# Two-layer convolution: the second image's last four chunks get their statistics from a quadratic form, and two weight loads are issued earlier

## The chip, the core and the metric

The kernel runs on one core of one Trainium2 chip. The metric is device time in microseconds (us): the median of 3 runs, and beside it one profiled execution from which all rows below are taken. Engines are named as the profile names them: PE (TensorE, matmul), PEld (its weight loads), DVE (VectorE), ACT (ScalarE), POOL (GpSimd), SP (SyncE, which here only issues DMAs).

## What is computed

Layer 0 is a bottleneck block with a deformable 3x3 convolution; the change touches it only in the order of two weight loads. Layer 1, cut to what matters, is this, for two images of 1024 channels and 64x64 pixels:

```python
t = jnp.einsum('oc,bchw->bohw', Wt, x)      # 512 channels
p = jnp.einsum('oc,bchw->bohw', Wp, x)
g = jnp.einsum('oc,bchw->bohw', Wg, x)
y = _rbf_kernel(t, p, g)                    # att0 + att1*t + att2*t**2 per image, att from sums of p**k * g
z = jnp.einsum('oc,bchw->bohw', Wz, y)      # 1024 channels
mu = jnp.mean(z, axis=(1, 2, 3), keepdims=True)
var = jnp.mean((z - mu) ** 2, axis=(1, 2, 3), keepdims=True)
zn = (z - mu) * jax.lax.rsqrt(var + EPS)
zn = zn * gn_w[None, :, None, None] + gn_b[None, :, None, None]
return zn + x
```

So no output of an image can be finished before mean and variance over all of that image's z are known.

## The kernel before

The pixels are worked in 16 chunks of 512 (8 for each image). A 1024-channel tensor of one chunk is 8 tiles of 128 channels x 512 pixels, so z is 128 tiles, counted by i; chunk zc holds the tiles 8*zc to 8*zc+7. The matrix products are done in two parts: each operand is split into a rounded high part and the rest, and `product` (L194 to L196) issues three matmuls, high by high, high by low, low by high. ACT makes the high part and DVE the low one.

The program is a hand-written list for each engine, with semaphores between them; every engine works its list strictly in order. The stages in time:

- convolutions of layer 0, then projections of layer 1 (the weights of the projections are loaded into three staging buffers by `stage`, L464 on SP, split by ACT at L699 and DVE at L1081). While the first projections run, DVE and ACT work through a long list of gathered tiles.
- the z stage. For chunk zc+1, while z of chunk zc runs: POOL loads t into the single buffer `tb` (L658), ACT scales it (`y_scale`, L903), DVE multiplies (`y_square`, L1320), ACT rounds y to `yh` (`y_high`, L915), DVE takes the rest `yl` (`y_low`, L1324). PE makes a tile of z with 4 x 3 matmuls into one of six PSUM banks; the first and the last two tiles of a chunk are done as pairs (`z_pair`). ACT copies the tile from its bank to SBUF (`z_evict`, L968), and DVE takes its statistics (`stats`, L1367). z stays in SBUF in a ring of 71 tiles.
- when an image's 64 tiles have their statistics, DVE, PE and ACT combine them (`fin_mean`, L1618 and L1622 on PE, `fin_std`, `fin_scale`). Then for each tile DVE adds the saved input (`add_x1`, L1402), ACT adds the bias (`fin`, L976), SP stores 256 KB (`store_out`, L560).
- for the first image the 64 additions are spread over the second image's z by `adds_by` (L157): after tile 64+x, max(x-3, 3(x-5)/2) of them are done, so 1.5 for each tile. A tile's bias on ACT comes one tile later. Their inputs come through four buffers `xs` of 256 KB (`load_xs`, L549); on SP the load of xs i+4 stands directly ahead of the store of tile i.
- for the second image everything from L1372 on comes behind the last tile of z; its inputs come as pairs of tiles (512 KB) into 16 buffers `xb` and `xt` (`load_x1`, L554).

## Time and profile before

| | us |
|---|---|
| median of 3 runs (lowest, highest) | 2355.5 (2354.93, 2360.31) |
| the profiled execution | 2341.42 |
| its span, first to last instruction | 2339.6 |
| first matmul of z to the end of the last, about | 1900.7 to 2264.4 |
| from there to the end | 75.2 |

A span counts from the first to the last instruction. A row of the timeline has the start, the duration, the engine, the line and what it writes and reads; a bracket tells how long the engine was idle before it and what it waited for. Matmuls overlap in the records: a 128x512 one lasts 0.39 us and the next starts 0.23 us after it. What one costs is the distance of two starts. "SPq" and "POOLq" are the issuing of DMAs.

### The profile page before, as it was taken

How to read it: one execution, taken by the hardware profiler on the slowest of the kernel's cores; microseconds unless marked ns; L12 is line 12 of the kernel's file. 1: busy time of each engine (PE TensorE's matmuls, PEld its weight loads, DVE VectorE, ACT ScalarE, POOL GpSimd, SP SyncE). 2: the span in 40 equal slices, each digit the busy share in tenths (PEclk: the TensorE clock that was granted, in tenths of full speed). 3: DMA queues.
4: the chain of work that ended last, by engine and by line, in shares of the span. 5: the costliest groups of instructions: out<-in, count | busy, mean ns of one | idle time of the engine just before them, and what ended most of it. 6: DMA issues, size and time to landing. Idle time of an engine off the chain costs nothing.

```text
span 2339.6 us, 29804 instructions
## 1 busy us (share of the span) xinstructions
PE 2236.2 (96%) x10252; PEld 1853.8 (79%) x10252; DVE 1573.2 (67%) x3177; ACT 1252.9 (54%) x2432; POOL 794.7 (34%) x706
## 2 busy tenths in 40 slices
PE   8999999999989999999999999999999999999970
PEld 6888888888868888888888888888888878887750
DVE  4222324766788898889888988898884334467855
ACT  6444545453455565556555655565563324456745
POOL 0100003434224665566566766676651000000000
PEclk9999999999999999999999999999999999999985
DMA  9998889999998998898889889998883111118869
GB/s 304 313 314 287 303 299 376 399 401 393 403 374 290 315 333 312 305 327 315 304 308 326 307 305 312 318 322 307 310 319 128 72 54 36 54 52 295 313 229 388
DMA packets 289824, 667.97 MB, mean 286 GB/s; under 512 B 27112, under 2 KB 101608, under 8 KB 283528
## 3 DMA queue, kind: packets, MB, share of 16 engines
q0 software_dynamic: 88048, 322.81, 39.3%
q1 hardware_dynamic: 172536, 262.59, 31.5%
q10 hardware_dynamic: 29088, 80.67, 9.3%
q8 instruction: 81, 1.33, 0.2%
q14 instruction: 71, 0.58, 0.1%
HBM read 435.47 MB, written 230.49 MB: 285 GB/s over the span
## 4 chain that ended last, share of the span: by engine, by line
PE 87%; DVE 5%; DMA 4%; SPq 2%; ACT 1%; issue 1%; POOL 0%; ACTq 0%; DVEq 0%
PE bank L194 23%; PE bank L196 23%; PE bank L195 23%; PE bank L1458 5%; PE bank L1459 5%; PE bank L1460 5%; DVE z L1402 2%; PE bank L1476 2%; DMA xs<-x 1%; DMA g<-vwide,tbl 1%; SPq L458 1%; SPq L462 1%; PE bank L1500 0%; PE bank L1484 0%; DMA xt<-x 0%
## 5 line engine op out<-in xcount | busy, mean ns | idle before, releaser
L643 POOL DMA_INDIRECT g<-vwide,tbl x512 | 605.4, 1182 | 509.9 <-DVE a L1030 214.4
L194 PE MATMUL bank<-x1h,wlh 128*128 128x512 f32 x1536 | 603.1, 393 | 3.5 <-DVE x1l L1292 3.5
L196 PE MATMUL bank<-x1h,wll 128*128 128x512 f32 x1536 | 600.1, 391 | 0.0
L195 PE MATMUL bank<-x1l,wlh 128*128 128x512 f32 x1536 | 599.3, 390 | 0.0
L1030 DVE SCALAR_TENSOR_TENSOR a<-g,tbl,a 128x256 f32<-128x256 f32 x1224 | 529.0, 479 | 25.0 <-DMA g<-vwide,tbl 18.0
L670 ACT ACTIVATE g<-g,tbl 128x256 f32<-128x256 f32 x1008 | 427.1, 499 | 217.9 <-DMA g<-vwide,tbl 179.3
L194 PEld LDWEIGHTS bank<-x1h,wlh 128*128 128x128 f32 x1536 | 288.8, 188 | 64.0 <-issue 3.7
L196 PEld LDWEIGHTS bank<-x1h,wll 128*128 128x128 f32 x1536 | 288.6, 188 | 62.2
L195 PEld LDWEIGHTS bank<-x1l,wlh 128*128 128x128 f32 x1536 | 289.0, 188 | 60.7
L748 ACT ACTIVATE vb<-bank 128x512 f32<-128x512 f32 (+1 forms) x320 | 174.2, 554 | 191.1 <-PE bank L1460 161.4
L1458 PE MATMUL bank<-w2h,o1h 128*128 128x512 f32 (+1 forms) x640 | 236.7, 370 | 0.0
L1459 PE MATMUL bank<-w2l,o1h 128*128 128x512 f32 (+1 forms) x640 | 235.8, 368 | 0.0
L1460 PE MATMUL bank<-w2h,o1l 128*128 128x512 f32 (+1 forms) x640 | 235.4, 368 | 0.0
L1085 DVE TENSOR_TENSOR xl<-xin,xh 128x1024 fp32r<-128x1024 f32 x64 | 78.2, 1225 | 222.7 <-ACT xh L720 222.6
L194 PE MATMUL bank<-yh,wzh 128*128 128x512 f32 x512 | 203.3, 397 | 5.5 <-DVE yl L1324 4.2
L196 PE MATMUL bank<-yh,wzl 128*128 128x512 f32 x512 | 202.0, 395 | 0.0
L195 PE MATMUL bank<-yl,wzh 128*128 128x512 f32 x512 | 201.6, 394 | 0.0
L647 POOL DMA_INDIRECT g<-vone,tbl x128 | 153.6, 1200 | 131.4 <-DVE a L1014 100.7
L658 POOL DMA_DIRECT2D tb<-t x16 | 8.7, 544 | 448.9 <-DVE yl L1324 438.2
L1367 DVE BATCH_NORM_STATS2 zst<-z 128x6 f32<-128x512 f32 x128 | 87.4, 690 | 103.7 <-ACT z L968 103.6
L1011 DVE TENSOR_TENSOR a<-a,g 128x512 f32<-128x512 f32 x224 | 153.7, 686 | 0.3 <-ACT g L670 0.3
L1014 DVE TENSOR_TENSOR a<-a,g 128x512 f32<-128x512 f32 x224 | 153.7, 686 | 0.0
(154 smaller groups left out, 3206.6 us busy)
## 6 DMA issues: line engine op xcount, KB each, us to landing
vwide<-vb SPq DMA_DIRECT2D x256, 256.0 KB, 5.8
vwide<-vb SPq DMA_DIRECT2D x112, 512.0 KB, 5.3
xf<-in_x SPq DMA_DIRECT2D x32, 1024.0 KB, 6.4
x<-xf ACTq DMA_DIRECT2D x32, 1024.0 KB, 7.0
out<-z SPq DMA_DIRECT2D x128, 256.0 KB, 5.1
xin<-in_x ACTq DMA_DIRECT2D x54, 512.0 KB, 5.5
t<-ts ACTq DMA_DIRECT2D x64, 256.0 KB, 5.0
tb<-t POOLq DMA_DIRECT2D x16, 1024.0 KB, 5.8
```

The lines of the kernel that those rows point to most:

```text
L194: nc.tensor.matmul(out, wh, xh, start=first, stop=False)
L195: nc.tensor.matmul(out, wh, xl, start=False, stop=False)
L196: return nc.tensor.matmul(out, wl, xh, start=False, stop=last)
L643: pool.indirect_dma_start(slot[:].rearrange("p a c -> p (a c)"), None, d["vwide"][img], bass.IndirectOffsetOnAxis(ap=at[:, i, tap(u), 0:1] ...
L670: ins = nc.scalar.activation(slot[:, c, :], slot[:, c, :], ACT.Copy, scale=TBL[p % 3][:, 1, tap(u), w:w + 1])
L748: nc.scalar.activation(VB[g % NVB][:, 0:n, a, :], RING[count % 4][:, 0:n * CMID].rearrange("p (t c) -> p t c", c=CMID), ACT.Copy).then_inc ...
L1011: nc.vector.tensor_tensor(acc, acc, slot[:, 0:2 * CMID], ALU.add).then_inc(half_done, 1)
L1014: nc.vector.tensor_tensor(acc, acc, slot[:, 2 * CMID:4 * CMID], ALU.add).then_inc(g_used[1], 1)
L1030: ins = nc.vector.scalar_tensor_tensor(out=acc, in0=slot[:, c, :], scalar=scale, in1=acc, op0=ALU.mult, op1=ALU.add)
L1458: nc.tensor.matmul(out, oh, W2H[:, k, lo:hi], start=k == 0, stop=False)
L1459: nc.tensor.matmul(out, oh, W2L[:, k, lo:hi], start=False, stop=False)
L1460: last = nc.tensor.matmul(out, ol, W2H[:, k, lo:hi], start=False, stop=k == KMID - 1)
```

## The change

1. SP issues `stage(5)` and `stage(6)`, two weight loads of 512 KB for the projections, ahead of the stores of the last quarter chunk of v instead of behind them.
2. The statistics of z of the second image's last four chunks (12 to 15) are taken without z. With M = Wz^T Wz (512x512), the sum of z squared is the sum of y times My, and the sum of z is the column sums of Wz by the sums of y. So:
   - ahead of z tile 88 (`M_AT`), PE makes M from Wz in 8 `piece`s of 12 matmuls (free sizes 512, 384, 256 and 128, three each; only the upper blocks), with Wz loaded again in another layout (`raw`, 2 MB, by POOL) and split by ACT (`piece_high`) and DVE (`piece_low`); M itself is split too (`product_high`, `product_low`), and six 128x128 blocks are mirrored by transposes.
   - z of chunks up to 11 is computed as before ("held" tiles). Behind tile 95, `quadratic` runs 4 times (one for each of chunks 12 to 15) with 32 matmuls, and DVE multiplies and sums the results (`q_sum`). `y_high` of these passes adds a sum (`accum_out`).
   - then `fin_mean_1`, `partition_sums`, `fin_var_1`, `fin_std_1`, `fin_scale(1)` make the second image's factors. Then z of chunks 12 to 15 is computed for real, for which t is loaded and y made a second time. These 32 "direct" tiles are neither copied nor measured: `add_x1` reads the PSUM bank. Each odd tile is followed by 4 additions, 2 held tiles and 2 direct ones.
3. The first image's additions are all done before that (`added_by` in place of `adds_by`): 11/6 for each tile from x=4, 10 over the 8 pieces, 2 for each tile of chunk 11.
4. The squares of y of `yc` 9 to 15 are done by POOL (`q_square`) and no longer by DVE; a second buffer `tb2` serves two of the quadratic chunks.
5. `split_low` of Wz also sums its columns (8 small reductions, `wbar`).

```diff
+    for i in range(ZT, M_AT):
+        x = i - ZT
+        cum.append(11 * (x - 4) // 6 + 1 if x > 3 else 0)
+    for p in range(MPIECES):
+        cum.append(cum[-1] + 1 + (p % 4 == 3))
+    for i in range(KIN):
+        cum.append(cum[-1] + 2)
+    for k in range(KCP * QUADS_Z):
+        cum.append(cum[-1] + 1)
...
                     for t in range(TILES):
+                        if s == ALLC and t == TILES - 1:
+
+                            stage(5)
+                            stage(6)
                         store_v(s - 1, t)
...
-            for w in range(5, 2 + GROUPS):
+            for w in range(7, 2 + GROUPS):
...
+            def q_square(yc, k):
+                pool.wait_ge(u_done, KCP * yc + k + 1)
+                nc.gpsimd.tensor_tensor(tb(yc)[:, k, :], UB[k % 2][:], tb(yc)[:, k, :], ALU.mult).then_inc(u2_done, 1)
...
+            for qi in range(QUADS_Z):
+                yc = FIRST_Q + qi
+                for k in range(KCP):
+                    y_scale(yc + 1, k)
+                for k in range(KCP):
+                    y_high(yc + 1, k)
+                for k in range(KCP):
+                    fins(E_Q + KCP * qi + k)
...
+            for qi in range(QUADS_Z):
+                yc = FIRST_Q + qi
+                for k in range(KCP):
+                    y_square(yc + 1, k)
+                for k in range(KCP):
+                    adds(E_Q + KCP * qi + k)
+                for o in range(KCP):
+                    q_sum(qi, o)
+                for k in range(KCP):
+                    y_low(yc + 1, k)
...
+            def quadratic(qi):
+                yc = FIRST_Q + qi
...
+                for k in range(KCP):
+                    pe.wait_ge(yh_done, KCP * yc + k + 1)
+                    for o in range(KCP):
+                        nc.tensor.matmul(q_bank(qi, o)[:], MH[k][:, 128 * o:128 * o + 128], YH[:, k, :], start=k == 0, stop=False)
+                        last = nc.tensor.matmul(q_bank(qi, o)[:], ML[k][:, 128 * o:128 * o + 128], YH[:, k, :], start=False, stop=k == KCP - 1)
+                    last.then_inc(q_done, 1)
```

On SP, at the end of layer 0, `in_wl` is the weight of the projections and `v_ev` the eviction of a v tile. Before:

```order
L456 DMA vwide<-vb_103 128x512 [waits v_ev]
L457 DMA vwide<-vb_103 128x256
L458 DMA vwide<-vb_103 128x256
L462 DMA vone<-vb_103 128x256 x2
L462 DMA vone<-vb_104 128x256 [waits v_ev]
L462 DMA vone<-vb_104 128x256
L473 DMA stage_165<-in_wl 128x1024 [waits wl_done]
L473 DMA stage_163<-in_wl 128x1024 [waits wl_done]
L473 DMA stage_164<-in_wl 128x1024 [waits wl_done]
```

and now:

```order
L561 DMA stage_171<-in_wl 128x1024 [waits wl_done]
L561 DMA stage_169<-in_wl 128x1024 [waits wl_done]
L544 DMA vwide<-vb_109 128x512 [waits v_ev]
L545 DMA vwide<-vb_109 128x256
L546 DMA vwide<-vb_109 128x256
L550 DMA vone<-vb_109 128x256 x2
L550 DMA vone<-vb_110 128x256 [waits v_ev]
L550 DMA vone<-vb_110 128x256
L561 DMA stage_170<-in_wl 128x1024 [waits wl_done]
```

Two of the three loads moved ahead of seven stores.

On ACT, around the end of chunk 10 (L968 and L1110 are `z_evict`, L976 and L1124 are `fin`, L915 and L1054 are `y_high`, L903 is `y_scale`). Before:

```order
L915 ACTIVATE yh<-tb,coef_80 128x512 [waits z_done,u2_done]
L968 ACTIVATE z_198<-bank 128x512 [waits out_done7,z_done]
L976 ACTIVATE z_205<-z_205,fb_84 128x512 [waits sum_done]
L976 ACTIVATE z_206<-z_206,fb_84 128x512 [waits sum_done]
L968 ACTIVATE z_199<-bank 128x512 [waits out_done0,z_done]
L976 ACTIVATE z_207<-z_207,fb_84 128x512 [waits sum_done]
L968 ACTIVATE z_200<-bank 128x512 [waits out_done1,z_done]
L976 ACTIVATE z_208<-z_208,fb_84 128x512 [waits sum_done]
```

and now, with the first pieces of Wz (`mph`):

```order
L1054 ACTIVATE yh<-tb,coef_86 128x512 [waits z_done,u2_done]
L1110 ACTIVATE z_204<-bank 128x512 [waits out_done7,z_done]
L1124 ACTIVATE z_219<-z_219,fb_90 128x512 [waits sum_done]
L1124 ACTIVATE z_220<-z_220,fb_90 128x512 [waits sum_done]
L1110 ACTIVATE z_205<-bank 128x512 [waits out_done0,z_done]
L1124 ACTIVATE z_221<-z_221,fb_90 128x512 [waits sum_done]
L1124 ACTIVATE z_222<-z_222,fb_90 128x512 [waits sum_done]
L1142 ACTIVATE mph_276<-raw_273 128x512 [waits out_done1,raw_in0]
L1124 ACTIVATE z_223<-z_223,fb_90 128x512 [waits sum_done]
L1142 ACTIVATE mph_277<-raw_273 128x512 [waits out_done3,raw_in0]
```

The first piece stands behind the last two evictions of the chunk and four biases.

On DVE, behind the last held tile (L1593 `stats`, L1697 `add_x1`, L1623 `q_sum`, L1550 `y_low`); before, stats and additions alternate here to the end of z. Now:

```order
L1593 BN_STATS zst<-z_213 128x6 [waits z_ev]
L1697 SCALAR_TENSOR_TENSOR z_250<-z_250,fa_88,xs_181 128x512 [waits xs_in1]
L1697 SCALAR_TENSOR_TENSOR z_251<-z_251,fa_88,xs_182 128x512 [waits xs_in2]
L1697 SCALAR_TENSOR_TENSOR z_252<-z_252,fa_88,xs_183 128x512 [waits xs_in3]
L1623 ISA sq,qs<-bank,sq,qs 128x512 [waits fin_ready,yl_done,q_done]
L1623 ISA qs 128x1
```

The last addition of the first image stands ahead of the first `q_sum`, and everything of the second image behind them.

## Rows read from the trace of the kernel before

**Rows 1.** The page's first table and clock row: busy us (share) xcount; tenths in 40 slices

```profile
PE 2236.2 (96%) x10252; PEld 1853.8 (79%) x10252; DVE 1573.2 (67%) x3177; ACT 1252.9 (54%) x2432; POOL 794.7 (34%) x706
...
PEclk9999999999999999999999999999999999999985
```

**Rows 2.** Busy us by stretch: start:end, length, PE PEld DVE ACT POOL, clock, DMA share, GB/s

```profile
690.00:700.00 10.00, 4.33 (x20) 3.25 (x18) 9.34 (x19) 8.00 (x18) 7.33 (x7) 0.98 0.99 375
700.00:707.00 7.00, 5.15 (x13) 4.10 (x14) 6.96 (x14) 5.46 (x11) 4.14 (x5) 0.54 0.98 376
...
2178.00:2201.00 23.00, 22.74 (x98) 18.11 (x97) 18.15 (x28) 17.65 (x29) 0.54 (x1) 1.00 0.90 320
```

**Rows 3.** The same view over the z stage and the tail behind it

```profile
1900.70:2264.40 363.70, 359.29 (x1542) 288.56 (x1542) 212.33 (x325) 195.77 (x312) 7.56 (x14) 1.00 0.44 151
2264.40:2339.60 75.20, 1.18 (x4) 1.00 (x4) 47.60 (x75) 43.61 (x66) 0.00 (x0) 0.51 0.92 349
```

**Rows 4.** Groups from 1800 on: shapes, count, busy us, mean ns, idle before

```profile
L976 ACT ACTIVATE z<-z,fb 128x512 f32<-128x512 f32 x128 | 87.2, 719 | 12.4 <-DVE z L1402 12.3
L968 ACT ACTIVATE z<-bank 128x512 f32<-128x512 f32 x128 | 75.0, 593 | 131.6 <-PE bank L196 122.6 <-DMA out<-z 7.9
...
L1320 DVE TENSOR_TENSOR tb<-ub,tb 128x512 f32<-128x512 f32 x64 | 44.0, 688 | 5.9 <-ACT ub L903 5.6
...
L1303 DVE CUSTOM_DVE_ANT_0 gs<-bank,gs,sums 128x512 f32<-128x512 f32 x6 | 4.5, 751 | 0.2
...
L877 ACT ACTIVATION_READ_ACCUMULATOR gs<-bank 128x1 f32 x5 | 1.0, 195 | 0.0
```

**Rows 5.** Timelines of PE: the start of a chunk of z, and half-wide matmuls

```profile
2217.81 0.39 PE L196 MATMUL bank<-yh,wzl 128*128 128x512 f32 x1
2219.50 0.47 PE L194 MATMUL bank<-yh,wzh 128*128 128x512 f32 x1 [1.30 <-DVE yl L1324]
...
400.41 0.28 PE L1460 MATMUL bank<-w2h,o1l 128*128 128x256 f32 x1
400.53 0.28 PE L1458 MATMUL bank<-w2h,o1h 128*128 128x256 f32 x1
```

**Rows 6.** Timelines of DVE and PE where a weight comes late

```profile
675.70 1.23 DVE L1081 TENSOR_TENSOR wll<-stage,wlh 128x1024 fp32r<-128x1024 f32 x1 [8.27 <-ACT wlh L699]
...
693.95 0.39 PE L196 MATMUL bank<-x1h,wll 128*128 128x512 f32 x1
701.85 0.79 PE L194 MATMUL bank<-o2h,w3h 128*128 128x512 f32 x1 [7.51 <-DVE o2l L1179]
```

**Rows 7.** Timeline of SP there, and the landing times of all stage loads

```profile
659.16 1.29 SPq L456 DMA_DIRECT2D vwide<-vb  x1
...
668.38 1.86 SPq L473 DMA_DIRECT2D stage<-in_wl  x3
...
DMA to landing us min/median/max: 3.4/6.4/12.6
```

**Rows 8.** Timeline of DVE around late inputs, and DVE's waits from 2117 to 2224

```profile
2192.21 1.41 DVE L1402 SCALAR_TENSOR_TENSOR z<-z,fa,xs 128x512 f32<-128x512 f32 x2
...
2203.58 0.75 DVE L1402 SCALAR_TENSOR_TENSOR z<-z,fa,xs 128x512 f32<-128x512 f32 x1 [2.92 <-DMA xs<-x]
...
2207.31 0.75 DVE L1402 SCALAR_TENSOR_TENSOR z<-z,fa,xs 128x512 f32<-128x512 f32 x1 [2.38 <-DMA xs<-x]
...
DVE z L1402 <- DMA xs<-x: 21.7, 16, 3.1
```

**Rows 9.** DMA issues from 2128 to 2224: count, KB each, median us to landing

```profile
xs<-x SPq DMA_DIRECT2D x49, 256.0 KB, 4.4
tb<-t POOLq DMA_DIRECT2D x5, 1024.0 KB, 8.6
```

**Rows 10.** The only compute row of POOL over a whole tile, in its groups

```profile
L593 POOL MEMSET ao<- 128x512 f32 x1 | 0.5, 525 | 0.3 <-POOLq L1671 0.3
```

**Rows 11.** Timeline of SP at the end

```profile
2332.66 1.95 SPq L560 DMA_DIRECT2D out<-z  x3
```

More of the change, by code:

```diff
@@ L310, in program, with q_bank, tb, tb_user @@
     PT, PM = BANK[0], BANK[1]
+    def q_bank(qi, o):
+        return ((ZB[0], ZB[1], ZB[2], ZB[3]), (ZB[4], ZB[5], PT, PM))[qi % 2][o]
+    def tb(yc):
+        return TB2 if yc in (FIRST_Q + 1, FIRST_Q + 3) else TB
+    def tb_user(yc):
+        return max((i for i in range(yc) if tb(i) is tb(yc)), default=None)
+    def t_ready(eng, yc):
+        eng.wait_ge(t2_in if tb(yc) is TB2 else t_in, 16 * sum(1 for i in range(yc + 1) if tb(i) is tb(yc)))
+    def z_slot(i):
+        return i % ZRING if i < DIRECT else 48 + (i - DIRECT) % DIRECTS
+    def mirrored(b):
+        return (PT[:, 0:128], PT[:, 128:384], PM[:, 0:384])[b - 1]
+    def raw_piece(p):
+        run = next(r for r, (lo, hi) in enumerate(RAW_RUNS) if lo <= p < hi)
+        return RAW[run][:, p - RAW_RUNS[run][0], :]
     def o2_tiles(n):
@@ new lines, in fins, with out_of, piece_high @@
+            def fins(e):
+                for j in range(added(e - 2), added(e - 1)):
+                    fin(j)
+            def out_of(tile):
+                act.wait_ge(out_done[tile % NOUT], 16 * (tile // NOUT + 1))
+            def piece_high(p):
+                run = next(r for r, (lo, hi) in enumerate(RAW_RUNS) if lo <= p < hi)
+                act.wait_ge(raw_in[run], 16)
+                if p < 2:
+                    out_of((25, 27)[p])
+                else:
+                    act.wait_ge(mm_done, GROUPS * ALLC + p - 1)
+                nc.scalar.activation(MPH[p % 2][:], raw_piece(p), ACT.Copy).then_inc(wh_done, 1)
@@ new lines, in mirror_high @@
+            def mirror_high():
+                act.wait_ge(tr_done, TILES * ALLC + KCP - 1)
+                for b in range(1, KCP):
+                    nc.scalar.activation(MH[b][:, 0:128 * b], mirrored(b), ACT.Copy).then_inc(wh_done, 1)
+            for i in range(DIRECT):
+                zc, k = divmod(i, KIN)
+                if i == M_AT:
+                    for p in range(MPIECES):
+                        piece_high(p)
+                        fins(E_M + p)
+                    product_high()
+                if k == KIN - 2:
+                    for kk in range(KCP):
+                        y_high(zc + 1, kk)
+                z_evict(i)
+                if i == M_AT + 2:
+                    mirror_high()
+                if 2 <= k < 2 + KCP:
+                    y_scale(zc + 1, k - 2)
+                if i == ZT + 3:
+                    fin_std()
+                if i >= ZT:
+                    fins(event(i))
@@ L1628, in _ @@
                     pe.wait_ge(xr_done, KIN * ALLC)
+                if KIN * zc == M_AT:
+                    for p in range(MPIECES):
+                        piece(p)
+                if zc == FIRST_Q:
+                    for qi in range(QUADS_Z):
+                        quadratic(qi)
                 for m in range(KIN):
```

394 lines of the change are left out of this document (306 added, 88 removed).

## The prediction

> **What bounds the kernel now.** I read the page's first table and its clock row first [rows 1]. PE is busy for 96% of the span, at the full clock nearly throughout; only the last slices show a lower one. So up to the end of z the kernel runs at PE's pace, and what is left to win is where PE stands still. The stretches [rows 3] show where: z takes 363.7 us, of which PE is busy for 359.3, and behind it come 75.2 us in which PE does next to nothing. There the DMA share is 0.92: 64 stores of 256 KB go out and the last inputs come in. The second place is one stop of 7.51 us at 693.95 [rows 6]. It also cost clock: in the 7 us behind it the granted clock was 0.54 [rows 2]. From 690 to 707 there began 20 + 13 = 33 matmuls; at 0.227 us each, 17 us hold 75, so the stop cost 42 x 0.227 = 9.5 us. Inside z the stops are short (1.30 us at one start of a chunk, with the clock staying full) [rows 5].
>
> The sum below is made against the span of 2339.6 us. The profiled execution took 1.8 us more than that and was 14.1 us below the median of the runs; I take the difference over to the median unchanged.
>
> **Part 1, the two weight loads.** DVE idled 8.27 us for a piece of weight that ACT could not round before the load landed [rows 6]. SP issued that load at 668.38, behind the seven stores that begin at 659.16 [rows 7]. Behind this point DVE is busy without a break up to the work for which PE stops at 693.95, so what DVE wins here PE gets back, up to its 7.51 us. Now two loads are issued at about 659.2. Stage loads take 3.4 to 12.6 us to land, 6.4 in the median [rows 7]; the DMAs are nearly full there (0.99 a little later, [rows 2]), so I take 8 to 9: landed at 668, split by ACT and DVE at about 669, DVE 6.5 us earlier. PE's stop shrinks to about 1 us, which by [rows 5] costs no clock: **-8 us**. At the slow end of 12.6 us DVE wins 2.7, and PE gets 3 back; the whole stop would be 9.5. The seven stores are 1 us later, and nothing near waits for them. Behind it PE's share of 96% and its full clock [rows 1] leave no other wait to fall into before z.
>
> **Part 2, the tail.** Of the 75.2 us [rows 3] there stays what the last two tiles need: two additions of 0.75 us (DVE, from the bank), one bias of 0.72 [rows 4], and from the last issue of a store to the end 5 us (2332.66 + 1.95 = 2334.6 against 2339.6, [rows 11]). That is 7.6 us: **-67.6 us**. It holds only if DVE, ACT and the DMAs keep up with the 32 direct tiles, 32 x 12 x 0.2325 = 89.3 us of PE (359.29 us for 1542 matmuls [rows 3] make 0.233 from start to start). For each chunk of 22.3 us DVE has 16 additions at 0.67 from start to start and 8 operations for y at 0.64, 16 us; ACT 16 biases at 0.63 and 8 operations for y, 15.5 us. DMA has 64 stores (16.8 MB), 18 of the 32 pairs of inputs (9.4 MB, the other 14 are loaded before) and three loads of t (3.1 MB): 29.3 MB in 89.3 us is 328 GB/s, below the 349 of the tail and its 0.92 share [rows 3]. So I expect no backlog.
>
> **Part 3, M.** A piece is three matmuls each of 512, 384, 256 and 128 columns. 512 cost 0.2325 [rows 3] and 256 cost 0.12 (400.41 to 400.53, [rows 5]); 384 lies between at 0.18, and for 128 I take 0.11, little under the 256. That is 3 x 0.64 = 1.93 us, eight times 15.4, and 0.7 for the six transposes: **+16.1 us** (if a narrow matmul cost as much as a full one, 22.3 + 0.7). ACT has 0.6 + 1.25 x 0.65 us for each piece, DVE 0.7 + 1.25 x 0.67: both under 1.93 (0.65 and 0.67 are the durations less what the next one overlaps: two additions in a row take 1.41, one 0.75, [rows 8]).
>
> Its start has no cover. When tile 87 is done, ACT still has one y_high, two evictions and four biases ahead of the first piece, as the listing of the change shows, and DVE one y_low, four additions and two stats. Again from start to start: DVE 0.1 + 0.7 (ACT's y_high, [rows 4] has 0.72 for the like) + 0.75 + 4 x 0.67 + 2 x 0.6 (stats) = 5.4, and the piece itself 0.69: PE stops for 6.1 us. The stop of 7.51 us cost 2 us of clock on top (9.5 in all), so **+8.1 us**. Cover comes from nowhere; if the raw load lands late it is more.
>
> **Part 4, the quadratic passes.** 4 x 32 x 0.2325 = 29.8 us of PE. Between two passes ACT has four y_scale (I take 0.71, as the bias has 0.719 [rows 4]), of which each but the first two waits for POOL's square two before it (two buffers), four y_high with the accumulator read of 0.195 [rows 4], and in the first pass four biases. No compute of POOL of this kind is in the trace. The nearest rows: DVE does it in 0.688 [rows 4]; POOL's memset writes 128x512 in 0.525 [rows 10], and three such streams (two read, one written) are 1.58. I take 1.3, nearer to the row of POOL's own, with 0.7 and 1.6 as ends and more as a rival. Then y_scale goes at 0.71 + 2 x 1.3 + 0.71 = 4.0 us for four, y_high at 0.84 each 3.4, biases 2.5. Pass 1 can begin 9.6 us behind the end of tile 95 (y_high 0.9, two evictions at 0.5 from start to start [rows 4] and four biases, 4.5 together; then y_scale 4.2 and the first y_high 0.9), where PE is done with pass 0 at 7.4: stop 2.2. Pass 2 begins 10.1 later (7.4 + 2.7 stop), pass 3 about 8.2 later (0.8 stop, since the biases are gone). Then DVE must do four q_sum, 0.75 each [rows 4] and 0.09 for the sum's read, and the first y_low, 0.75 as an addition [rows 8], before PE may begin tile 96: 4.3 us. Sum 29.8 + 5.7 + 4.3 = 39.8, and 2 for the clock behind the last stop: **+41.8 us**. With a square of 0.7 it is 4 less, with 1.6 it is 2 more. partition_sums costs 0.6; the chain of small operations of fin_mean_1 (about 3 us) lies beside tiles 96 and 97.
>
> The Trainium skill, GPSIMD Engine Reference, section 3.1, says that an elementwise operation of two tensors takes this engine about 2.6 cycles per element at 1.2 GHz, which makes an estimate of 1.1 us for 512; by that the sum would be 1 us lower. No row here shows it.
>
> **Part 5, the first image's additions.** Before, 1.5 fall on a tile, now 1.83. Their inputs come through four buffers, and on SP the load of tile i+4 stands ahead of the store of tile i, which waits for its bias. So five additions can't take less than one round: bias, two issues, landing (4.4 us in the median, while the 1 MB of t takes 8.6 and holds the others up [rows 9]), addition. This ring already limits: DVE waited 21.7 us in 16 stops for xs, 2.92 and 2.38 close together [rows 8]. From the addition at 2193 the next five, around the load of t, took until 2207.3, 14.3 us, [rows 8]; the others come about 1.3 us apart (0.67 for the addition, as much for the stats and squares between): 14.3 + 7 x 1.3 = 23.4 for 12 additions, and 98 matmuls began in 23 us [rows 2], 96 make a chunk. With 14.7 it is 26.9, so 3.5 us more for each chunk of 8, 2 and a half chunks long; then 10 during M, which has room, and 16 in chunk 11 (28.6 against 23.4). In all up to 14 to 18 us. Against that stand PE's six banks, which let ACT be some 3 us late without a stop, and POOL's squares, which take 4 x 0.6 us a chunk off DVE. I take **+7 us**, ends 0 and 18.
>
> **Sum.** -8 - 67.6 + 16.1 + 8.1 + 41.8 + 0.6 + 7 = -2.0 us. The 8 small reductions with the split of Wz (0.6 us each) come ahead of z, where DVE has few tasks left: nothing, or 1 us if PE's first tiles wait for them. Predicted: 2355.5 - 2.0 = 2353.5 us.
>
> **The rivals.** (A) Slower, by POOL: its squares take 2.6 us or more, or DVE's own two-input operations slow down beside them. From 1.9 us a square on, the four of a pass (7.6) exceed the pass itself (7.44). At 2.6 each pass is 2.6 us longer on ACT's list, and with stops then above 4 us the clock falls between passes too: 3 x (2.6 + 2) = +14 us, 2367. The same skill page (GPSIMD Engine Reference, section 1) says that the engine shares its SBUF interfaces with VectorE; no run here shows what that costs. For it: no row of such an instruction. Against: one pass has slack elsewhere. (B) Slower, by the xs ring: part 5 in full (+18 instead of +7), 2364; it decides once a chunk with 14.7 additions takes over 25 us. For it speaks [rows 8]; against it, PE loses only about 1 us a chunk today. (C) Faster: the ring costs nothing, since DVE is relieved and its idle time was harmless, and the entry into M is covered better (3 us instead of 8): -2 - 7 - 5 = -14, 2341.5. (D) The loads moved up change nothing, as they land behind the stores that are already queued: +8, 2361.5.
>
> **How the numbers follow.** A measurement of this kernel can tell about 0.3% (7 us) from no change. My forecast (within 8 us of -2) has 0.45, of which 0.30 is within 7 us of nothing, 0.10 faster and 0.05 slower. A 0.12 (0.10 slower, 0.02 same), B 0.13 (0.08 slower, 0.05 same), C 0.24 (0.22 faster, 0.02 same), D 0.06 (half same, half slower). Faster 0.32, same 0.42, slower 0.26. The range leaves 0.2 out: 2338 to 2368.
>
> **What would show it.** After the change: the stop behind 694 is under 2 us and z begins about 8 us earlier (part 1); the last z matmul is followed by under 10 us (part 2); the pieces come every 1.9 to 2 us, with a stop of 6 us and a fallen clock ahead of them (part 3); from the first to the last quadratic matmul some 35.5 us, then 4.3 us of nothing (part 4); POOL's square near 1.3 us; from tile 68 to 87 some 58 us of z against 56 without stops (part 5). It is wrong if PE stops for more than 10 us at M, if the direct tiles wait for xt or for free banks, or if the tail keeps more than 15 us of stores.

## The result, and the profile after

The changed kernel takes 2370.5 us (median of 10 runs, 2359.3 to 2381.5), the kernel before 2351.1 in the same sessions (10 runs, 2344.0 to 2360.5). The ratio is 1.0079 with a 95% interval of 1.0058 to 1.0100: 0.8% or 18.6 us slower. Predicted were 2353.5 and a range of 2338 to 2368.

The changed kernel's first table and clock row, as [rows 1]. PE is 61 us busier; 53 of them are M and the quadratic passes (18.2 and 35.0 in the next view), part of them at half clock. The clock row shows one dip, in the slice from 2127 to 2186 with the stop ahead of M, and no slow end. The lower clock in the passes (0.86 in the next view) is spread over slices that the row still gives as 9.

```profile
PE 2297.1 (97%) x10480; PEld 1900.6 (80%) x10480; DVE 1591.7 (67%) x3219; ACT 1265.1 (54%) x2466; POOL 831.8 (35%) x741
...
PEclk9999999999999999999999999999999999998999
```

Busy times by stretch, as [rows 3] (start:end, length, PE PEld DVE ACT POOL, clock, DMA share, GB/s): z up to tile 87; the stop ahead of M; M; chunk 11; the quadratic passes; the direct tiles; the tail.

```profile
1908.76:2160.92 252.16, 248.45 (x1061) 199.61 (x1062) 136.38 (x204) 126.04 (x200) 21.24 (x22) 0.99 0.29 99
2160.92:2175.26 14.34, 0.40 (x2) 0.00 (x0) 9.75 (x15) 8.86 (x15) 3.46 (x5) 0.61 1.00 357
2175.26:2193.64 18.38, 18.19 (x97) 16.66 (x97) 11.52 (x17) 8.84 (x15) 0.00 (x0) 0.84 0.97 349
2193.64:2216.70 23.06, 23.06 (x105) 18.67 (x105) 15.42 (x24) 18.25 (x37) 6.16 (x5) 1.00 0.73 253
2216.70:2266.18 49.48, 35.03 (x129) 27.57 (x128) 35.40 (x65) 31.11 (x59) 17.55 (x15) 0.86 0.71 267
2266.18:2357.76 91.58, 91.57 (x386) 73.29 (x386) 64.40 (x107) 56.41 (x87) 1.65 (x3) 0.98 0.91 344
2357.76:2363.40 5.64, 0.00 (x0) 0.00 (x0) 0.88 (x2) 1.43 (x2) 0.00 (x0) 0.89 0.25 93
```

The tail is gone as forecast and the direct tiles run without a wait (their 384 matmuls take 91.6 us, as those of tiles 96 to 127 took before). What is too long is the stop ahead of M, 14 us at a full DMA share (more than the 10 us that the prediction named as a sign of its being wrong), and the passes, 49.5 us with PE busy for 35. PE's long stops there, in its timeline:

```profile
2175.26 0.80 PE L247 MATMUL bank<-mph 128*128 128x512 f32 x1 [13.95 <-DVE mpl L1600]
...
2229.89 0.76 PE L1974 MATMUL bank<-yh,mh 128*128 128x512 f32 x1 [5.77 <-ACT yh L1056]
...
2244.24 0.77 PE L1974 MATMUL bank<-yh,mh 128*128 128x512 f32 x1 [4.01 <-ACT yh L1056]
...
2266.18 0.47 PE L247 MATMUL bank<-yh,wzh 128*128 128x512 f32 x1 [4.67 <-DVE yl L1550]
```

DVE's timeline ahead of M tells what the first piece (`mpl`) stands behind. Two additions wait for their inputs, one between the stats of tiles 86 and 87, ahead of the first piece, and one between the first piece and the second:

```profile
2169.28 0.69 DVE L1593 BATCH_NORM_STATS2 zst<-z 128x6 f32<-128x512 f32 x1
2173.26 0.75 DVE L1697 SCALAR_TENSOR_TENSOR z<-z,fa,xs 128x512 f32<-128x512 f32 x1 [3.30 <-DMA xs<-x]
2173.93 0.69 DVE L1593 BATCH_NORM_STATS2 zst<-z 128x6 f32<-128x512 f32 x1
2174.53 0.67 DVE L1600 TENSOR_TENSOR mpl<-raw,mph 128x512 fp32r<-128x512 f32 x1
2177.83 0.75 DVE L1697 SCALAR_TENSOR_TENSOR z<-z,fa,xs 128x512 f32<-128x512 f32 x1 [2.62 <-DMA xs<-x]
```

The DMA issues of 2160 to 2177 (count, KB each, median us to landing) say why. POOL issues raw only at 2162.19, behind the last square of chunk 11's `y`, then t; the inputs that SP issues beside them land after 10 us, where [rows 9] had 4.4:

```profile
xs<-x SPq DMA_DIRECT2D x7, 256.0 KB, 10.4
raw<-in_wn POOLq DMA_DIRECT2D x1, 1024.0 KB, 8.4
tb<-t POOLq DMA_DIRECT2D x1, 1024.0 KB, 9.1
```

So the late addition is only the last of the delays. The first part of raw landed at 2170.6, and ACT took it up at once:

```profile
2170.61 0.63 ACT L1142 ACTIVATE mph<-raw 128x512 fp32r<-128x512 f32 x1 [0.50 <-DMA raw<-in_wn]
```

With 0.6 us of ACT and 0.7 of DVE the first piece could not have been ready before about 2171.9, which is 10.6 of the 14 us; the addition that waited adds the other 3.3. Why POOL came to raw so late is read from ACT's waits from 2137 to 2176: POOL's squares wait for ACT's `y_scale`, and ACT stood behind biases whose additions were late.

```profile
ACT z L1124 <- DVE z L1697: 11.0, 6, 2.9
```

The change from the start of z on, from the starts of PE's matmuls in the two profiled executions (us):

| | before | after | difference | predicted |
|---|---|---|---|---|
| tiles 0 to 85 | 242.0 | 246.8 | +4.8 | +7 |
| tiles 86, 87, stop and M | 7.4 | 38.1 | +30.7 | +23.5 |
| tiles 88 to 95 with the mirroring | 22.7 | 23.1 | +0.4 | +0.7 |
| quadratic passes to tile 96 | 0 | 49.5 | +49.5 | +42.4 |
| tiles 96 to 127 | 91.6 | 91.6 | 0 | 0 |
| tail | 75.3 | 5.7 | -69.6 | -67.6 |
| sum | 438.9 | 454.7 | +15.8 | +6.0 |

Ahead of z the changed kernel is 2.9 us ahead at about 840 us, compared matmul by matmul (predicted 8), and then loses 10.9 us up to z. 6 us of that are short stops of PE without a cause that the profile shows; the last section comes back to them. So comparisons of z below count from z's first matmul (1900.75 before, 1908.76 after), and whole kernels are compared by ratio.

### The profile page after: what moved, and what is told of

Same layout as the page of the kernel before. It is cut to its first block, busy times and chain, and to the rows that moved or that the text cites. A ratio compares the mean times of both kernels' runs of the same rounds, so it can differ in the third digit from the quotient of the medians.

```text
span 2363.4 us, 30452 instructions
## 1 busy us (share of the span) xinstructions
PE 2297.1 (97%) x10480; PEld 1900.6 (80%) x10480; DVE 1591.7 (67%) x3219; ACT 1265.1 (54%) x2466; POOL 831.8 (35%) x741
## 4 chain that ended last, share of the span: by engine, by line
PE 89%; DMA 4%; DVE 2%; issue 1%; SPq 1%; ACT 1%; POOL 0%; DVEq 0%; ACTq 0%; POOLq 0%
PE bank L247 23%; PE bank L248 23%; PE bank L249 23%; PE bank L1785 5%; PE bank L1786 5%; PE bank L1787 5%; DMA xs<-x 2%; PE bank L1803 2%; DMA g<-vwide,tbl 1%; PE bank L1827 1%; PE bank L1811 1%; DVE z L1697 0%; DMA vwide<-vb 0%; SPq L545 0%; DMA vone<-vb 0%
## 5 line engine op out<-in xcount | busy, mean ns | idle before, releaser
L1508 DVE TENSOR_TENSOR x1l<-xf,x1h 128x512 fp32r<-128x512 f32 x128 | 84.0, 689 | 92.3 <-ACT x1h L998 87.2
```

## The experiments

All ratios are to the kernel before, measured beside it, with a 95% interval. "z to end" is from z's first matmul to the end in the profiled execution, 438.9 us before and 454.7 after. It is one execution for each kernel: where the work is nearly the same (438.9, 437.8 with only the loads moved, 440.1 with t in parts) it differs by 1 to 2 us.

### The parts alone, in the kernel before

**Only the two weight loads.** `stage(5)` and `stage(6)` ahead of the last `store_v`, nothing else.

> The kernel before with nothing but the two weight loads issued ahead of the last seven stores of v. The prediction's part 1: -8 us (ratio 0.9966), the PE stop behind 693 shrinks from 7.51 to about 1 us. The trace theory (from the profile of the changed kernel, where that stop was still 6.74 us, the one at 655 went from 3.55 to 2.31 and the one at 779 from 1.40 to 0.84): -3 us (ratio 0.9988), that is within what can be measured. Rival: the loads moved up change nothing at all, 0 us, and what the changed kernel showed there was variation.

Measured: 1.0018 (0.9995 to 1.0042), so no gain, and -8 us (0.9966) is excluded. PE's stop of 7.51 us [rows 6] is still there:

```profile
701.08 0.79 PE L194 MATMUL bank<-o2h,w3h 128*128 128x512 f32 x1 [7.34 <-DVE o2l L1182]
```

DVE's waits from 655 to 702 (what waited, for what: us in total, times, longest), before and here, show where its 8.27 us of [rows 6] went:

```profile
DVE wll L1081 <- ACT wlh L699: 8.3, 1, 8.3
DVE x1l L1292 <- ACT x1h L869: 1.9, 1, 1.9
DVE a L1030 <- DMA g<-vwide,tbl: 0.7, 1, 0.7
```

```profile
DVE wll L1084 <- ACT wlh L702: 6.5, 2, 4.5
DVE x1l L1295 <- ACT x1h L872: 2.5, 1, 2.5
DVE a L1033 <- DMA g<-vwide,tbl: 2.1, 1, 2.1
```

One wait of 8.3 has become two for two weights (4.5 and 2.0), and DVE now waits longer for its other operands, those from ACT and the gathered tiles: 10.9 us in all before, 11.1 now. The load itself gained less than its place in the order: SP issued it at 657.49 and not at 668.38, and ACT, which waited for it, began at 670.19 and not at 674.61. So it took about 12.7 us to land and not 6.2.

**Only the denser additions.**

```diff
-    return max(0, min(64, max(x - 3, 3 * (x - 5) // 2)))
+    return min(64, 11 * (x - 4) // 6 + 1) if x > 3 else 0
```

> The kernel before with nothing changed but the table of the first image's additions: 11/6 for each tile from x=4 instead of 3/2. The prediction's part 5: +7 us (ratio 1.003), ends 0 and +18. The trace theory: the z tiles 0 to 87 of the changed kernel took 3.0 us more than before, with 24 of them under the denser table, so over 34 tiles +4 us here (1.0017), with one or two PE stops of some 3 us for a bank that ACT evicts late. The rival B of the prediction: the four-buffer ring of inputs in full, +14 to +18 us (1.006 to 1.0077).

Measured: 1.0062 (1.0034 to 1.0090), +14.6 us; z to end 448.4. So the rival, the ring in full, was right. The three chunks behind tile 72 take 26.5, 27.0 and 25.9 us (23.5, 24.2, 22.7 before); at the end of each PE stops for 2.0 to 4.0 us, and at the two longer stops the clock falls to half. DVE's waits from 2113 to 2217:

```profile
DVE z L1402 <- DMA xs<-x: 23.4, 20, 4.6
```

**Only the squares on POOL** (chunks 9 to 15: `y_square` returns, POOL multiplies behind each `load_t`).

> The kernel before with nothing changed but the squares of y of chunks 9 to 15, which POOL does instead of DVE. The prediction: a square near 1.3 us and nothing lost, 0 us (1.000). The trace theory: a square is 1.39 us, DVE's additions beside it take some 0.88 us instead of 0.75, but PE's pace covers both: 0 to +2 us. Rival A of the prediction, in the z stage: DVE slowed beside POOL falls behind and PE stops for it at each chunk, 7 times 1 to 2 us, +7 to +14 us (1.003 to 1.006).

Measured: 1.0028 (1.0005 to 1.0050), z to end 440.1, so slightly slower. Groups of 2090 to 2165, first of the kernel before, then of this one:

```profile
L1402 DVE SCALAR_TENSOR_TENSOR z<-z,fa,xs 128x512 f32<-128x512 f32 x32 | 23.5, 746 | 11.3 <-DMA xs<-x 11.3
```

```profile
L1408 DVE SCALAR_TENSOR_TENSOR z<-z,fa,xs 128x512 f32<-128x512 f32 x25 | 22.9, 926 | 6.6 <-DMA xs<-x 6.6
L662 POOL TENSOR_TENSOR tb<-ub,tb 128x512 f32<-128x512 f32 x12 | 17.2, 1436 | 37.0 <-ACT ub L907 37.0
```

A square takes POOL 1.44 us here, twice DVE's 0.69 of [rows 4], and DVE's additions go from 0.746 to 0.926 us on average. For each chunk POOL takes 4 x 0.64 = 2.6 us of squares off DVE, and the 12 additions take 12 x 0.18 = 2.2 us more. The average hides two kinds: of this run's 64 additions the 37 that ran beside no square took 0.74 us, the 27 that ran beside one 1.22. The Trainium skill, GPSIMD Engine Reference, section 1, says that this engine shares its SBUF interfaces with VectorE; the trace agrees and puts this number on it.

**Both.**

> The kernel before with the denser additions and POOL's squares of chunks 9 to 15 together (alone they gave 1.0062 and 1.0028). If DVE's busy time plus its waiting for inputs is what makes a chunk long, POOL takes 2.8 us of each chunk from DVE and gives back about 1.3 (additions that run beside a square take longer): 1.003 to 1.005, less than the denser additions alone. If the two costs have nothing to do with each other: 1.009.

Measured: 1.0059 (1.0045 to 1.0073), z to end 451.9. Neither the sum of the two (1.009) nor a relief: POOL's squares don't help the denser additions.

### What makes the ring slow, in the kernel before with the denser additions

**Half the bytes of an input** (columns 0 to 255 of each input but the first four; a part of x is then not added).

> The kernel before with the denser additions (ratio 1.0062 by themselves), and of each input of the first image's additions but the first four only half the columns loaded: 128 KB instead of 256 KB, the rest of the buffer is old. Bandwidth theory (with 14.7 additions for each chunk of 22.4 us, their loads and stores of 0.52 MB and 1.05 MB of t are 8.8 MB, which at the 345 GB/s that such stretches reach takes 25 us): now 6.9 MB or 307 GB/s, so no PE stop behind tile 72 but the start of a chunk, ratio 1.000 to 1.001. Rival, the order of issues in the ring of four buffers makes the stops: a load still stands behind a store that waits for its bias, and at least half of the 14.6 us stays, 1.003 or more.

Measured: 1.0042 (1.0019 to 1.0065), z to end 444.3; stops of 2.9 and 3.6 us at chunk starts stay. The DMA share in these chunks is 0.80 to 0.81 now, so full DMAs are not the whole reason.

**Loads two further ahead of the stores on SP.**

```diff
-            for i in range(len(XS)):
+            for i in range(len(XS) + 2):
                 load_xs(i)
...
-                if i + len(XS) < ZT:
-                    load_xs(i + len(XS))
+                if i + len(XS) + 2 < ZT:
+                    load_xs(i + len(XS) + 2)
```

> The kernel before with the denser additions, and SP issuing the inputs two loads further ahead of the stores, all bytes as they were. Bandwidth theory: the DMAs are full (share 0.93 to 0.95), so the order of issues changes little, 1.005 to 1.007. Ring theory: the stops go, 1.001 to 1.002.

Measured: 1.0057 (1.0032 to 1.0083), z to end 448.3. The order of loads and stores on SP is not the reason.

**t in four parts over 9 us** (POOL issues part k behind `y_low` k and, for parts 2 and 3, behind two or three evictions of the chunk).

> The kernel before with the denser additions, and the 1 MB of t of each chunk loaded in four parts of 256 KB that POOL issues over the chunk's first 9 us instead of at once. Burst theory (with four buffers an input has two tiles, 5.6 us, to come; it takes 4 to 5 us, but about 8 for those beside the 1 MB of t, and these few are what the lists stand behind): inputs land in 5 us or less throughout, the PE stops at chunk starts fall under 2 us, ratio from 1.0062 to 1.001. Rival, the ring is too short at this density with any landing time over 4 us (the halved inputs took away only about a third): 1.004 to 1.006.

Measured: 1.0069 (1.0057 to 1.0081), z to end 453.1. The burst is not the reason either: the longest landing falls from 8.5 to 7.8 us, the mean stays.

**The same parts of t in the kernel before.**

> The kernel before with nothing changed but t in four parts issued over the chunk's first 9 us. Burst theory: the stops of 1 to 1.7 us at three chunk starts of the second image go, with them the 4.6 us that late inputs cost this kernel (438.9 us of z and tail against 434.3 with the dense table and no late inputs), ratio 0.998 to 0.999, and it would be faster than both kernels. Rival: t in parts comes later for ACT's scaling and gives back what it wins, 1.000 to 1.001.

Measured: 1.0002 (0.9993 to 1.0011). No gain.

What the slow ones have in common is read from issues, landings and additions between tiles 72 and 86, in means (us): from the end of addition i to the issue of load i+4, from there to landing, and from the start of addition i to that of i+4 (the rest is 0.7 for the addition and 0.4 to 0.9 of waiting for DVE). With four buffers a chunk of 14.67 additions lasts 14.67/4 of that round:

| | issue | landing | round | 14.67/4 rounds | chunks, mean of three |
|---|---|---|---|---|---|
| dense | 0.5 | 5.4 | 7.1 | 26.2 | 26.5 |
| half the bytes | 0.6 | 4.5 | 6.8 | 24.9 | 25.5 |
| loads ahead | 0.5 | 5.2 | 7.3 | 26.8 | 26.3 |
| t in parts | 0.5 | 5.5 | 7.1 | 26.2 | 27.0 |
| dense, POOL | 0.4 | 5.6 | 7.2 | 26.6 | 26.8 |

That the last two columns agree is mostly counting, since the round holds DVE's waiting too. What bounds the chunk is the part that no list can shorten: in the kernel before 12 additions in 22.4 us leave 7.5 us for a round; now 14.67 leave 6.1, while issue, landing and addition alone take 0.5 + 5.4 + 0.7 = 6.6. That gives 24.2 us; the other 2 or so come from landings that are uneven (up to 8.5 us) and waiting for DVE. None of these edits took enough off the landing. More buffers would be the direct test; it wasn't tried, since the memory of the stage is full, so that four buffers are the limit is worked out and not shown by an edit.

**No later inputs.** The loads behind the first four are left out, and every addition reads one of these four; additions and stores stay.

```diff
-                    v.wait_ge(xs_in[i % len(XS)], 16 * (i // len(XS) + 1))
+                    v.wait_ge(xs_in[i % len(XS)], 16)
```

> The kernel before with the denser additions and, as in the run before, without the loads of inputs behind the first four. Waiting theory: DVE is busy for 20 of the 22.4 us of a chunk and keeps up when nothing is late, so the 14.6 us that the denser additions cost are gone, 1.000. Rival, DVE's (and ACT's) own work is too much at 14.7 additions a chunk: stops of 2 us or more at chunk starts stay, 1.003 or more.

Measured: 0.9986 (0.9977 to 0.9995), z to end 434.3, the chunks 23.1, 22.4 and 22.3 us. DVE has the same operations as in the dense kernel and keeps up. So the 14.6 us come from the inputs, and the own work of DVE and ACT is no part of them; the kernel before pays 4.6 us of this kind itself. The edit also takes 60 loads of 256 KB from the DMAs, and which part of the gain is an addition's own wait and which the lighter traffic it doesn't tell.

### The changed kernel

**No later inputs here** (the same edit).

> The changed kernel without the loads of the first image's inputs behind the first four: the additions and the stores are all made, but every addition reads one of the first four inputs and waits for none behind them. Waiting theory (the lists of DVE and ACT stand in order behind additions whose inputs are late, and that is all that came on top of my sum): the stop ahead of M falls from 13.95 us to the 6 of my prediction or, since POOL still issues raw behind its squares, 8; from the first quadratic pass to tile 96 it is 42 to 43 us instead of 49.5; z up to tile 86 is as in the kernel before; ratio 1.001 to 1.002. Own-work theory (POOL's squares, the length of the lists and t make the stops between the passes): those 49.5 us stay above 47, ratio 1.004 or more.

Measured: 0.9990 (0.9981 to 0.9999), z to end 434.8. The stop ahead of M, in PE's timeline, and the stretch from the first quadratic matmul to tile 96:

```profile
2152.61 0.80 PE L247 MATMUL bank<-mph 128*128 128x512 f32 x1 [5.52 <-DVE mpl L1598]
```

```profile
2193.80:2236.85 43.05, 32.37 (x129) 25.39 (x128) 32.76 (x61) 30.51 (x57) 18.05 (x15) 0.92 0.72 259
```

These are 5.5 us where the prediction had 6.1, and 43.05 where it had 42.4. POOL's squares are as slow as before, and the lists as long: the waiting theory holds, the own-work theory is out. Here too the DMAs have nearly 16 MB less to move, so it doesn't divide what an addition waits for itself from what raw and t gain. Raw shows both: POOL issues it at 2144.12, ahead of the last matmul of tile 87 (at 2162.19 in the changed kernel it was behind it), and its first part lands after 5.9 us and not 8.4.

**Squares back on DVE.**

> The changed kernel with the squares of y of 9 to 15 back on DVE, so that POOL computes nothing in z. Theory 1, POOL's squares and their place behind the load of t make most of the stops between the quadratic passes (5.8, 4.0 and 4.7 us in the changed kernel): the passes up to tile 96 take 43 us instead of 49.5, and the ratio to the kernel before falls from 1.0079 to about 1.005. Theory 2, DVE is the shorter resource there (a pass would then give it 4 squares at 0.69, 4 sums at 0.84 and 4 y_low at 0.75, 9.1 us against 7.44 of PE): nothing won, 1.008. Rival: without POOL's help DVE falls behind with the first image's additions in chunks 9 to 11, and it is slower, 1.010 or more.

Measured: 1.0083 (1.0050 to 1.0116); the passes 50.2 us. Nothing won and nothing lost, as theory 2 said. By itself the edit only says that four squares a pass cost as much on DVE as on POOL; that POOL wasn't what made the passes long is said by the run without later inputs, which keeps POOL's squares and takes 43.

**Loads two ahead of the stores.**

> The changed kernel, in which SP issues each input of the first image's additions (xs) two loads further ahead of the stores, so that no load stands behind a store that still waits for its bias. Ring theory (the round of addition, bias, store, load is what makes the denser additions cost the 14.6 us that they cost alone in the kernel before): DVE's 31 us of waiting for xs fall to under 15, the entry into M and the first quadratic pass lose 2 to 4 us each, ratio from 1.0079 to about 1.003. Rival, the DMAs' landing time is what DVE waits for and not the order on SP: 1.008. Third: with the stores later, tiles and raw loads that wait for a free slot come later, 1.010.

Measured: 1.0061 (1.0048 to 1.0075), z to end 452.2. The stop ahead of M is 10.2 us, the passes 48.0. It is the lowest ratio of the changed kernels with all their work, but the gain (2.5 us by z to end) is too small to be told from the 1.0079 with its interval.

**Half the bytes of an input** (as above).

> The changed kernel with half the columns of each input of the first image's additions but the first four (128 KB instead of 256 KB; the rest of the buffer is old). Bandwidth theory: from tile 72 to the first quadratic pass 7.3 MB fewer go through the DMAs, which are full there (shares 0.86 to 1.00). The raw loads land in 6 us instead of 8 to 11 and the inputs in under 5, the stop ahead of M falls from 13.95 to 8 or less (POOL still issues raw only behind its squares), the first stop between quadratic passes by 2 to 4, ratio 1.002 to 1.004. Rival, the order of the lists alone (raw behind squares, pieces behind biases) makes the stops: 1.007 to 1.008.

Measured: 1.0059 (1.0028 to 1.0091), z to end 447.6, the stop ahead of M 11.6 us where 8 or less was expected, the passes 46.9. By the ratio the theory's 1.002 to 1.004 is just inside the interval; z to end says 7 of the 20 us.

**The entry covered.** POOL loads the first seven eighths of raw directly behind `load_t(11)` instead of behind the squares; `piece_high` and `piece_low` 0 and 1 ahead of chunk 11's y; both evictions directly behind the last tile; the additions of tiles 86 and 87 later. Of it, on ACT:

```diff
+                if i == M_AT - 2:
+                    piece_high(0)
+                    piece_high(1)
+                    fins(event(i))
+                    for kk in range(KCP - 1):
+                        y_high(zc + 1, kk)
+                    z_evict(i)
+                    z_evict(i + 1)
+                    y_high(zc + 1, KCP - 1)
+                    continue
```

> The changed kernel with the entry into M covered: POOL issues the loads of raw some 20 us earlier, ACT and DVE split pieces 0 and 1 ahead of chunk 11's y, both evictions stand directly behind the last tile, and the additions of tiles 86 and 87 are done during M instead (12 there, 4 in the quadratic passes). Trace theory (the stop of 13.95 us and the half clock of 17 us behind it come from the late raw load and from the list of work ahead of the first piece): the stop falls to under 2 us and pieces begin 1.9 us apart at once, -14 us, ratio 1.002. Rival: 2 MB more on the DMAs during chunk 10 make xs late, and what M wins z loses: 1.006 to 1.008.

Measured: 1.0104 (1.0089 to 1.0119), z to end 462.7: slower than what it was meant to mend. The stop came down to 10.9 us only, and came back inside M:

```profile
2164.69 0.79 PE L247 MATMUL bank<-mph 128*128 128x512 f32 x1 [10.87 <-DVE mpl L1621]
...
2172.56 0.50 PE L247 MATMUL bank<-mph 128*128 128x512 f32 x1 [1.72 <-DVE mpl L1621]
...
2179.87 0.79 PE L247 MATMUL bank<-mph 128*128 128x512 f32 x1 [3.25 <-DVE mpl L1621]
```

DVE's timeline again has a late input ahead of the first and the last of these (ahead of the second it has three additions in a row):

```profile
2162.69 0.75 DVE L1718 SCALAR_TENSOR_TENSOR z<-z,fa,xs 128x512 f32<-128x512 f32 x1 [5.69 <-DMA xs<-x]
...
2178.47 0.75 DVE L1718 SCALAR_TENSOR_TENSOR z<-z,fa,xs 128x512 f32<-128x512 f32 x1 [3.54 <-DMA xs<-x]
```

**The entry covered, no later inputs.**

> The changed kernel with the entry into M covered (raw 20 us earlier, pieces 0 and 1 split ahead of chunk 11's y, evictions first, the additions of tiles 86 and 87 during M) and without the loads of inputs behind the first four. Waiting theory: the cover failed alone (1.0104) only because DVE and ACT stood behind late inputs, in the entry and again at pieces 4 and 5. Now the stop ahead of M is under 2 us and the pieces are 1.92 us apart, 6 to 8 us less than with the full entry: 0.998 to 0.999. Rival, the lists of DVE and ACT are too long around M for a cover in any case: pieces still come over 2.5 us apart, 1.002.

Measured: 0.9993 (0.9984 to 1.0002), z to end 435.9. So inputs were why the cover failed, but the cover isn't worth the 6 to 8 us expected of it even without them. The stop is 2.0 us instead of 5.5, others of 1.8 and 0.6 follow, half the clock comes behind them as well; from the start of tile 86 to that of tile 88 it is 28.3 us instead of 29.4. The passes take 2.3 us longer; the edit leaves them four of the first image's additions and not three, but that this is the reason isn't shown.

**POOL's squares ahead of its load of t.**

> The changed kernel in which POOL, in the quadratic passes, does the squares of a chunk ahead of the load of t that waits for the y_low of the chunk before (one wait of 5.0 us of ACT there). Theory: of the stops between passes (5.8, 4.0, 4.7 us) the middle one loses 3 to 4 us and with it the clock's 3 us behind it, -5 us, ratio 1.006. Rival, POOL's 4 x 1.39 us for squares and DVE's sums and y_low set the pace whatever the order: 1.008. The other side: the loads of t for the last passes come later, and the last stop grows, 1.009.

Measured: 1.0090 (1.0076 to 1.0103). The middle stop falls from 4.0 to 0.7 us as the theory said, and the next one opens at 7.8: t for the last pass is now issued behind seven loads of 512 KB on SP and lands 8.6 us later. That was the third expectation, and it decided: z to end is 459.2.

**All three.**

> The three edits of the runs before this one together. If entry, ring and POOL's order each cost what the theories say (14, 10 and 5 us, of which the ring's part overlaps the entry's): -20 to -25 us, ratio 0.998 to 1.000. If the DMAs are the limit around M, where 2 MB of weights, 1 MB of t and the xs compete: 1.004.

Measured: 1.0123 (1.0108 to 1.0139), z to end 462.5, where 1.000 or at worst 1.004 was expected. The stop ahead of M is down to 6.4 us, but pieces wait inside M and the passes take 52.6. So together the three edits win nothing.

**Squares first, loads ahead, and the seven pair loads held until that t has landed** (`sp.wait_ge(t2_in, 32)`).

> The changed kernel with SP's inputs two loads ahead, POOL's squares ahead of its next load of t, and the seven loads of 512 KB for the direct tiles held back until the t of the last quadratic pass has landed (that t took 8.6 us behind them, and with POOL's order alone the third stop was 7.8 us for it). Bandwidth theory: t lands in about 4 us, the stops at pass 2 and 3 fall under 2 us each and their half clock goes, the quadratic passes take 43 us instead of 49.5 and with what the ring's order gave, 1.003 to 1.004; the direct tiles, at a DMA share of 0.91 already, may give back up to 3 us. Rival: what is held back is missing behind tile 96, the direct tiles wait for their inputs, 1.007 or more.

Measured: 1.0095 (1.0061 to 1.0129), the passes 51.9 us. That t does land 5.2 us after its issue, but the issue stands behind POOL's squares (2256.19), and the next t meets the held loads and takes 8.1: the stops are 4.5, 5.5 and 6.0 us. The direct tiles did not miss their inputs (97.1 us from tile 96 to the end, 97.3 in the changed kernel), so the rival is out, and the theory too.

## Why the prediction was wrong

The forecast was -2.0 us, the result +18.6. By steps:

- **Part 2, the tail: right.** -69.6 against -67.6, no backlog in the direct tiles at 344 GB/s and a share of 0.91.
- **Parts 3 and 4, the work of M and of the passes and the lists around them: right in themselves.** Without late inputs the stop ahead of M is 5.5 us (6.1), the passes to tile 96 take 43.05 (42.4) with stops of 2.6, 3.7, 0.5 and 3.9 (2.2, 2.7, 0.8 and 4.3), pieces come 1.92 apart once the clock is back (1.93), and a square of POOL takes 1.39 us on average in the changed kernel (1.3). Two terms don't follow from their own parts: the third pass begins 7.6 us behind the second by the list given, not 8.2, and the last sums and `y_low` make 4.1, not 4.3. Together that is 0.8 us and changes nothing. Without late inputs on either side the change costs 434.8 - 434.3 = +0.5 us; my terms without parts 1 and 5 give -1.0.
- **Part 5, the first image's additions: the step that failed.** Late inputs, with the traffic that their loads make, cost the kernel before 438.9 - 434.3 = 4.6 us (its dense variant without late inputs as the measure) and the changed one 454.7 - 434.8 = 19.9: +15.3, where I took +7. The ratios of whole kernels, which don't hang on one execution, give the same within their intervals: 0.14% or 3.3 us and 0.89% or 20.8 us, a difference of 17.5. My own working from [rows 8] gave 14 to 18; I halved it for two reasons, and both fell. "PE's six banks, which let ACT be some 3 us late": banks bridge a delay once, but a ring that gives 14.67 additions in 26 us is late in every chunk. "POOL's squares, which take 4 x 0.6 us a chunk off DVE": with and without them the dense table costs the same (1.0059, 1.0062), since an addition beside a square takes 1.22 us and not 0.74. The same part also kept this cost inside z ("10 during M, which has room"). Only 4.8 us of it came there. The rest stood ahead of M and between the passes, because additions are in the same lists of DVE and ACT as the pieces and the y of the passes; the terms of parts 3 and 4 were worked out as if no input were ever late. Raw is a case of it: the prediction said that the stop would be longer if raw landed late, and gave that no price.
- **Part 1, the loads: wrong.** "What DVE wins here PE gets back": DVE's wait that I looked at fell from 8.3 to 4.5 us, and its waits together stayed at 11, with the DMA share at 0.99 [rows 2]. The kernel with the loads alone is not faster (1.0018). The term of the landing was too short as well: 8 to 9 us taken, about 12.7 measured, the slow end of [rows 7]. So the load came 4.4 us earlier and not 6.5, and PE got 0.2 us of it at its stop (7.34). Rival D said that nothing would change, at a chance of 0.06; its reason, that the loads land behind the queued stores, fits the landing, but the 4.4 us that were won were lost to later waits.
- **Sum.** -2.0, with part 1 at 0 and part 5 at +15.3, is +14.3. The measured +18.6 has an interval of about +-5 us, so the rest isn't told from nothing.
- **Rivals.** B (2364) has the right mechanism, and its condition came true (over 25 us for a chunk with 14.7 additions: 26.3 in the changed kernel, 26.5 with the denser additions alone); with D it gives 2372. A is half right: DVE does slow down beside POOL (0.75 to 0.88 us an addition in the changed kernel), but with the squares back on DVE the kernel is no faster, and its price of 14 us isn't seen. I treated the cases as alternatives; B and D both came true, and the range's upper end (2368) didn't hold two of them.

## What to carry to other kernels

Before work is packed more densely, divide the round of its buffers (issue, landing, use, from the trace) by their number. That is the least time from one use to the next, and neither free banks nor an idle engine shortens it. An operation that may wait for a transfer delays everything behind it in its engine's list, so its lateness has to be added at each exposed place of that list, not only in the stage where it is planned. Where the DMA share is near 1, expect that a load moved up is paid for by what it passes, and look at the sum of an engine's waits and not at the one wait that you meant to shorten.

## What the runs showed of the hardware that was not expected

- DVE's addition slows while POOL multiplies: 746 ns on average before, 882 to 926 with POOL's squares, single ones up to 1.88 us, and in the run of all three edits two in a row once took 6.3. POOL's multiplication takes 1.26 us at the shortest and 1.36 to 1.45 on average (28 in each of eleven runs). The Trainium skill's 2.6 cycles per element (GPSIMD Engine Reference, section 3.1; an estimate of 1.1 us) is below all of these. Groups of the changed kernel from 2090 to 2165:

```profile
L1697 DVE SCALAR_TENSOR_TENSOR z<-z,fa,xs 128x512 f32<-128x512 f32 x32 | 27.8, 882 | 16.0 <-DMA xs<-x 15.8
L767 POOL TENSOR_TENSOR tb<-ub,tb 128x512 f32<-128x512 f32 x12 | 17.2, 1430 | 42.8 <-ACT ub L1035 42.7
```

- It is not every operation of DVE that slows: the statistics, which read one tile, took 0.684 us beside a square and 0.687 beside none (13 and 53 in the run with POOL's squares alone). The timelines of DVE and POOL there show two additions that take 2.44 us together (1.41 in [rows 8]) and a statistics operation of the usual length:

```profile
2129.76 2.44 DVE L1408 SCALAR_TENSOR_TENSOR z<-z,fa,xs 128x512 f32<-128x512 f32 x2
2129.91 1.74 POOL L662 TENSOR_TENSOR tb<-ub,tb 128x512 f32<-128x512 f32 x1 [10.84 <-ACT ub L907]
2132.13 0.68 DVE L1373 BATCH_NORM_STATS2 zst<-z 128x6 f32<-128x512 f32 x1
2132.30 1.29 POOL L662 TENSOR_TENSOR tb<-ub,tb 128x512 f32<-128x512 f32 x1 [0.64 <-ACT ub L907]
```

- Half the bytes of a 256 KB load took only 0.9 of 5.4 us off its landing time beside other traffic.
- The clock's answer to a stop of PE varied: at a stop of 4.0 us in the dense kernel the granted clock was 0.5 for 6.8 us, at one of 2.3 us in the kernel with POOL's squares for 3.4 us, and at one of 2.5 us in the kernel with both it stayed full. At half clock a full matmul comes every 0.43 us instead of 0.23.
- Ahead of z the kernels differ at most in the two loads and the 8 small reductions, yet their z starts between 1898.5 and 1932.3 us in the profiled executions. In the late ones PE has many stops of 0.3 to 1.7 us for which the profile shows no cause. PE's waits from 800 to 1895 in the dense kernel with halved inputs (z from 1932.3); the kernel before has none there:

```profile
PE bank L194 <- issue: 6.5, 14, 1.1
PE bank L195 <- issue: 5.2, 7, 1.7
PE bank L196 <- issue: 3.7, 6, 0.9
```

The kernel before ranged from 2336 to 2344 us in three sessions and from 2342 to 2369 in the others, and the sessions ran on different chips. Whether these stops make this difference isn't shown, and what they are is open.
